# First attention of a gated two-layer block: the next group's key projection in step 3, GpSimd's weight split ahead of a group, the row maximum ahead of step 0's fill

## The reference, cut to what matters

```python
q = (layernorm(x) @ Wq + bq).reshape(B, L, 8, 4, 128)      # B=4, L=256, HID=512
k, v = split(ctx @ Wkv + bkv)                              # 8 key/value heads, 64 context tokens
scores = einsum('blkgd,bmkd->bkglm', q, k) * 128 ** -0.5   # 4 query heads share a key/value head
o = einsum('bkglm,bmkd->blkgd', softmax(scores), v)
x = x + tanh(g) * (o @ Wo + bo)
```

## Time and profile before

| | us |
|---|---|
| median of 3 runs | 1485.03 (1480.28 to 1485.92) |
| profiled execution, device time | 1481.86 |
| its span in the profile | 1480.1 |
| period of a group in the first attention | 40.83 |
| granted TensorE clock, mean of the span | 0.994 |

### The profile page before, as it was taken

The page is one execution under the profiler, slowest core; times in us unless marked ns, Lnnn a source line. Parts: engine busy times, 40 slices in busy tenths (PEclk is TensorE's granted clock), DMA queues, the critical chain, the costliest instruction groups (busy, mean ns, idle before and its releaser), DMA issues.

```text
span 1480.1 us, 24307 instructions
## 1 busy us (share of the span) xinstructions
PE 1394.9 (94%) x7976; PEld 1197.7 (81%) x7976; DVE 1055.5 (71%) x2794; ACT 799.7 (54%) x2210; POOL 464.1 (31%) x590
## 2 busy tenths in 40 slices
PE   4999999998999998999999999999999999999988
PEld 4888888897778877888878878878888888887777
DVE  7777777778632437787777777787787787787775
ACT  4777777776211315565555555555555555664642
POOL 3855555554963612111111111111121111112220
PEclk8999999999999999999999999999999999999999
DMA  4211212111321301001001001001001001010001
GB/s 192 72 62 53 71 71 71 59 69 44 105 68 43 124 1 72 1 1 72 1 1 71 0 1 71 0 1 71 0 1 71 0 1 71 0 43 13 1 8 50
DMA packets 14958, 63.96 MB, mean 43 GB/s; under 512 B 1760, under 2 KB 1760, under 8 KB 10656
## 3 DMA queue, kind: packets, MB, share of 16 engines
q1 hardware_dynamic: 14880, 63.07, 12.0%
HBM read 60.97 MB, written 2.10 MB: 43 GB/s over the span
## 4 chain that ended last, share of the span: by engine, by line
PE 39%; DVE 15%; issue 5%; ACT 4%; DVEq 0%; ACTq 0%
PE psum L57 12%; PE psum L59 11%; PE psum L58 11%; PE psum L1356 2%; PE psum L1450 2%; DVE mx L1041 2%; DVE pT_hi L1014 2%; DVE pT_lo L1010 1%; DVE w1o_lo L1003 1%; DVE p L1056 1%; DVE w1q_lo L1003 1%; ACT pT_hi L1212 1%; DVE dump L1034 1%; DVE oT_lo L1020 1%; DVE v_lo L1071 1%
## 5 line engine op out<-in xcount | busy, mean ns | idle before, releaser
L1289 ACT ACTIVATE p<-psum,nb,rq 128x320 f32<-128x320 f32 x256 | 155.2, 613 | 162.8 <-DVE nb L1045 162.8
L57 PE MATMUL psum<-w1q_hi,xnT_lo 128*128 128x512 f32 x288 | 120.9, 420 | 16.7 <-DVE v_lo L1065 9.0
L978 POOL TENSOR_TENSOR rk<-ssk,rms_eps 128x3 f32<-128x3 f32 x32 | 6.3, 196 | 350.7 <-DVE ssk L1082 350.7
L59 PE MATMUL psum<-w1q_hi,xnT_hi 128*128 128x512 f32 x288 | 113.7, 395 | 0.0
L1010 DVE TENSOR_TENSOR pT_lo<-psum,pT_hi 128x512 fp32r<-128x512 f32 x128 | 88.1, 689 | 35.9 <-ACT pT_hi L1212 34.1
L58 PE MATMUL psum<-w1q_lo,xnT_hi 128*128 128x512 f32 x288 | 112.9, 392 | 0.0
L1041 DVE TENSOR_REDUCE mx<-psum 128x2 f32<-128x640 f32 x128 | 105.0, 820 | 6.1 <-PE psum L59 0.5
L1253 ACT ACTIVATE q_raw<-psum 128x512 f32<-128x512 f32 x64 | 38.2, 597 | 123.6 <-PE psum L59 123.6
L363 DVE TENSOR_TENSOR VW_lo<-psum,VW_hi 64x512 fp32r<-64x512 f32 x128 | 88.0, 688 | 19.0 <-ACT VW_hi L459 17.4
L57 PE MATMUL psum<-w1o_hi,oT_lo 128*128 128x512 f32 x256 | 100.5, 393 | 0.0
L58 PE MATMUL psum<-w1o_lo,oT_hi 128*128 128x512 f32 x256 | 100.3, 392 | 0.0
(11 more groups left out here) (235 smaller groups left out, 4657.6 us busy)
## 6 DMA issues: line engine op xcount, KB each, us to landing
raw_q<-in_w0q SPq DMA_DIRECT2D x8, 1024.0 KB, 4.8
raw_o<-in_w0o SPq DMA_DIRECT2D x8, 1024.0 KB, 4.8
raw_q<-in_w1q SPq DMA_DIRECT2D x8, 1024.0 KB, 7.5
raw_o<-in_w1o SPq DMA_DIRECT2D x8, 1024.0 KB, 4.8
raw_kv<-in_w_gu SPq DMA_DIRECT2D x10, 512.0 KB, 3.6
raw_gu<-in_w_gu SPq DMA_DIRECT2D x10, 512.0 KB, 3.7
raw_kv<-in_w0kv SPq DMA_DIRECT2D x8, 515.0 KB, 3.3
raw_kv<-in_w1kv SPq DMA_DIRECT2D x8, 512.0 KB, 5.5
```

The source lines that it names most:

```text
L57: pe.matmul(out, w[1], m[0], start=start, stop=False)
L59: return pe.matmul(out, w[0], m[0], start=False, stop=stop)
L1289: last = act.activation(k.p1[:, tile, h, :], s_pair(j)[:, h % 2, :], ACT.Exp, bias=k.nb[:, i:i + 1], scale=k.rq[:, i:i + 1], accum_out=k.r ...
```

## The change

Four edits, all in the first attention. The key fill of the next group, ("kv", 0), moves from step 7 to step 3, on PE, ACT and DVE alike; the value fill stays in step 7. The numbers and banks of the fills follow the new order; the last group, which has no next fills, gets an order of its own. POOL copies the bias (now a sum with a tile of zeros) and makes kv hi and kv lo of the next group at the start of its body, ahead of the first scaling; only `q_last` stays behind it, and its wait changes from "all fills up to the group before are drained" to "(kv, 1) of the group now running is drained". On DVE the row maximum comes ahead of the fills in step 0, as in all the other steps.

```diff
-    NEXT_PREP = {7: [("kv", 0), ("kv", 1)], 8: [("wk", 0), ("wk", 1), ("wk", 2)], 9: ...
+    NEXT_PREP = {3: [("kv", 0)], 7: [("kv", 1)], 8: [("wk", 0), ("wk", 1), ("wk", 2)], 9: ...
...
-    ORDER = sum(OWN_PREP.values(), []) + sum(NEXT_PREP.values(), [])
+    ORDER = sum((OWN_PREP.get(s, []) + NEXT_PREP.get(s, []) for s in range(NT + 3)), [])
+    LAST_ORDER = sum(OWN_PREP.values(), [])
...
             if t == 0:                                        # next_ready
-                pool.wait_ge(kv_in, 16 * g + 16)
                 pool.wait_ge(q_in, 16 * g + 16)
-                pool.wait_ge(prep_free, HEAD + FILLS * (g - 1))
...
             if t == 0:                                        # next_split
-                bias_copy(pool).then_inc(bias_in, 1)
                 q_last_row(pool).then_inc(q_row_set, 1)
-                hi_piece("kv", 0)
-                hi_piece("kv", 1)
-            elif t == 1:
-                lo_piece("kv", g, 0)
-                lo_piece("kv", g, 1)
...
+        def split_kv(g, used):
+            pool.wait_ge(kv_in, 16 * g + 16)
+            pool.wait_ge(prep_free, used)
+            pool.tensor_tensor(k.bias[:, :], k.raw_kv[:, KVW:KVW + GH + 2], k.zeros[:, :], ALU.add).then_inc(bias_in, 1)
+            for i in range(CONV["kv"]):
+                hi_piece("kv", i)
+            for i in range(CONV["kv"]):
+                lo_piece("kv", g, i)
+
         def body(g, nxt):
+            if nxt:
+                first = isinstance(g, int) and g == 0
+                split_kv(g + 1, 2 if first else HEAD + FILLS * (g - 1) + ORDER.index(("kv", 1)) + 1)
...
-                if s == 0:                                    # vector, body
-                    for fill in fills:
-                        prep(base, fill)
                 if s < NT:
                     dve.wait_ge(s_full, n + 1)
                     dve.tensor_reduce(k.nb0[:, s % 2, :], by_head(s_bank[s % 2][:, 0:GH * CTX]), AX.X, ALU.max,
                                       negate=True).then_inc(nb_ready, 1)
-                if s > 0:
-                    for fill in fills:
-                        prep(base, fill)
+                for fill in fills:
+                    prep(base, fill, nxt)
```

More of the change, by code:

```diff
@@ L153, in attn0_phase @@
                 4: [("vw", 1, 1)], 5: [("vw", 2, 1)], 6: [("vw", 3, 1)]}
-    NEXT_PREP = {7: [("kv", 0), ("kv", 1)], 8: [("wk", 0), ("wk", 1), ("wk", 2)], 9: [("wk", 3), ("wk", 4), ("wk", 5)],
+    NEXT_PREP = {3: [("kv", 0)], 7: [("kv", 1)], 8: [("wk", 0), ("wk", 1), ("wk", 2)], 9: [("wk", 3), ("wk", 4), ("wk", 5)],
                  10: [("wk", 6), ("wk", 7), ("vw", 0, 0)]}
-    ORDER = sum(OWN_PREP.values(), []) + sum(NEXT_PREP.values(), [])
-    FILLS, OWN = len(ORDER), sum(map(len, OWN_PREP.values()))
+    ORDER = sum((OWN_PREP.get(s, []) + NEXT_PREP.get(s, []) for s in range(NT + 3)), [])
+    LAST_ORDER = sum(OWN_PREP.values(), [])
+    FILLS, OWN = len(ORDER), len(LAST_ORDER)
     HEAD = FILLS - OWN
@@ L171, in attn0_phase, with place @@
     arrived, hi_of, lo_of = {"kv": kv_in, "q": q_in, "o": o_in}, {"kv": kv_hi, "q": q_hi, "o": o_hi}, {"kv": kv_lo, "q": q_lo, "o": o_lo}
-    def place(base, fill):
+    def place(base, fill, nxt=True):
         if base is None:
@@ L177, in place @@
         else:
-            at, slot = base + ORDER.index(fill), HEAD + ORDER.index(fill)
+            i = (ORDER if nxt else LAST_ORDER).index(fill)
+            at, slot = base + i, HEAD + i
         return at, k.bank[slot % 3]
@@ L300, in gpsimd @@
         pool.memset(k.minus_half[:, :], -0.5)
+        pool.memset(k.zeros[:, :], 0.0)
         pool.wait_ge(ident0, 1)
@@ L345, in head_o_hi, with prep @@
             dve.tensor_copy(k.w_o[0][:, :], k.raw_o[:, :]).then_inc(o_hi, CONV["o"])
-        def prep(base, fill):
-            (at, bank), kind = place(base, fill), fill[0]
+        def prep(base, fill, nxt=True):
+            (at, bank), kind = place(base, fill, nxt), fill[0]
             dve.wait_ge(prep_hi, at + 1)
@@ L516, in tensor, with prep @@
     def tensor(pe):
-        def prep(base, fill, g):
-            (at, bank), kind = place(base, fill), fill[0]
+        def prep(base, fill, g, nxt=True):
+            (at, bank), kind = place(base, fill, nxt), fill[0]
             if not (isinstance(at, int) and at < 3):
@@ L552, in body @@
                 for fill in OWN_PREP.get(s, []):
-                    prep(base, fill, g)
+                    prep(base, fill, g, nxt)
                 for fill in NEXT_PREP.get(s, []) if nxt else []:
@@ L578, in body @@
                     if t == 0:
-                        pe.wait_ge(prep_free, base + ORDER.index(("vw", 3, 0)) + 1)
+                        pe.wait_ge(prep_free, place(base, ("vw", 3, 0), nxt)[0] + 1)
                     if t == 4:
-                        pe.wait_ge(prep_free, base + OWN)
+                        pe.wait_ge(prep_free, place(base, ("vw", 3, 1), nxt)[0] + 1)
                     if not (first and t < 2):
@@ L1743, in build @@
             k.w_q, k.w_o = pair(scope, "w0q", [QW]), pair(scope, "w0o", [QW])
-            k.bias, k.q_last = sb(scope, "bias", [GH + 2]), sb(scope, "q_last", [GH])
+            k.bias, k.q_last, k.zeros = sb(scope, "bias", [GH + 2]), sb(scope, "q_last", [GH]), sb(scope, "zeros", [GH + 2])
             k.kvT = pair(scope, "kvT0", [2, BATCH * CTX])
```

## The result

The changed kernel has a median of 1467.95 us (1465.57 to 1468.37, 4 runs) beside 1485.47 us (1480.28 to 1486.25, 4 runs) for the kernel before on the same chip. The ratio is 0.9888, 95% interval 0.9869 to 0.9907: 16.6 us faster by the ratio, between 14 and 19. The forecast was 1469 us. The profiled execution took 1468.23 us with a span of 1466.4; before it was 1481.86 and 1480.1.

What follows compares the result with a forecast made beforehand. PE's order of work sets the pace, with stops of 2.37 us a group to win. 6 x 1.92 + 1.0 + 1.37 = 13.9 us, taken from a mean of 1483.3, gives 1469 us; range for 8 in 10: 1462 to 1477.

Steps and rivals of the forecast that it cites:

- Gap A: PE's stop before S(2), behind tile 0's exponentials: 0.63 us a group, to go with the earlier row maximum.
- gap B: PE's stop between S(3) and tile 1's transposes, for pT lo: 1.74 us a group, to go with both edits.
- The new wait at the wk fill: PE's first wk fill would wait for POOL's last Wq lo piece: 0.45 us a group, about 0.95 in group 0.
- The rival without a new wait: At the wk fill POOL's piece comes early enough: 17.5 us gained, 1466 us; chance 0.10.
- The rival by which the time comes back later: Wq or wk drains hold PE nearly as long as was won: 0 to 5 us gained, near 1481; chance 0.09.
- POOL's split: About 3.9 us of kv work ahead of the first scaling, covered with 4 us; in group 0 no cover.
- the rival by which POOL blocks DVE: In steps 10 and 0 the split locks DVE out, delaying the maximum: +9.5 us, 1493; 0.05 for above 1483.
- the rival by which it fills nothing: ACT or DVE falls behind in step 3, PE waits one tile on: 7.8 us gained, 1475.5; chance 0.14.
- Group 7: The last group, without a key fill, gains 1.37 us by the earlier row maximum alone.
- the full group, 1.92 us: Gain of each of six groups: 2.37 us of PE's stops less 0.45 of wait at the wk fill.

Runs made afterwards that it cites:

- the tile last: Changed kernel with the tile of zeros allocated behind all others, so kvT, WK, VW, p and pT stand where they stood before: 1470.0 us, ratio 0.9896.
- the reordered one: Changed kernel with POOL's last Wq lo piece ahead of the first Wo hi piece at tile 6: 1463.14 us, ratio 0.9852.
- the kernel with the fill first: Changed kernel with the fill put back ahead of the row maximum in step 0: 1474.34 us.
- 128-byte tile: Changed kernel with a tile of zeros of 128 bytes a partition in place of 64: 1466.64 us, single run.
- all shifted: Kernel before the change with 64 bytes allocated ahead of all tiles: 1484.07 us, ratio 1.0001.
- the split late: Changed kernel with POOL's split of kv back behind the first two scalings, key fill in step 3: 1494.55 us, single run.
- the first padded kernel: Changed kernel with POOL's Wq lo piece moved first, plus 64 unused bytes ahead of w_kv and 64 ahead of w_q: 1465.25 us, ratio 0.9868.

## Why the prediction was right, step by step

**Both stops were caused as told.** Gap A and the larger part of gap B came from the late maximum, the rest of gap B could be filled: the maximum alone leaves 6.0 us of the 13.1 waited and gains 1.33 us a group where 1.37 was worked out; the key fill without the maximum leaves 0.1 us of gap B. With both, PE stops at neither. The margin for pT lo of tile 0 is 0.43 us (163.90 against 164.33), where 0.66 was worked out; PE also arrives earlier for being quicker. One tile on, 0.9 was worked out: pT lo of tile 1 ends at 167.10 and PE asks at 167.99.

**The new wait at the wk fill** was put at 0.45 us: PE is free at 181.38 (181.15 and one pace of 0.23), starts at 181.74, and the first matmul after it is slow by 0.11: 0.47. Two of its terms miss in opposite directions: POOL's piece ends at 181.69, so PE comes 0.31 us too soon where 0.23 was worked out, and it starts 0.05 us behind POOL's end where 0.12 was taken from group 0. Most of the first miss is PE's quicker pace again: with the tile last it is 0.25. In group 0 it was put at 0.95: 0.84 idle and about 0.1 of slow restart. The order of POOL's pieces, which takes this wait away, gives 0.51 back. The rival without a new wait fell for this kernel and is what the reordered one does. The rival by which the time comes back later fell too, since nothing but this wait is new.

**POOL's split** is covered in full groups by 4.38 us, where 4 was worked out. In group 0, where it has no cover, POOL's scaling holds the transposes by 0.36 us, as told, and they come at 44.88 (44.95). That the two times agree to 0.1 us means little: over the thirteen traces here they lie anywhere from 44.34 to 45.40. Its durations are the old ones (1.17, 2.56), and the drain of DVE beside it in group 0 is still 1.39 for two. So the rival by which POOL blocks DVE fell. The key fill brought back no wait one tile on: the rival by which it fills nothing fell.

**Group 7** gains by the maximum alone: from the first transposes of group 7, 16.82 us earlier, to the feed-forward, 17.43 us earlier, it is 0.61, where 1.37 - 0.63 = 0.74 was worked out. PE's wait for pT lo there is 1.0 us.

**The term that was mis-sized** is that of the full group, 1.92 us: it measured 2.45, and 2.05 where the tiles stay in their old places. The sum, cut at the first transposes of a group:

| | forecast | measured |
|---|---|---|
| up to group 1's first transposes (group 0's 1.0 and group 1's gap A, 0.63) | 1.63 | 2.11 |
| six full groups | 11.52 | 14.71 |
| from group 7's first transposes on | 0.74 | 0.61 |
| first attention | 13.9 | 17.4 |

Of the 3.5 us that were missed, 2.7 are PE's pace, shown by the kernel with the tile last: 0.40 in each of six groups, and 0.34 from group 0's first transposes to group 1's (39.31 against 38.97). The other 0.13 us a full group are no single error: cut at the transposes, no stretch of the group with the tile last is off the forecast by more than 0.04 us. The forecast took every matmul at the pace of before; the tile of zeros was costed at its 0.2 us sum on POOL, and not as something that moves what lies behind it.

**Where the agreement is luck.** The profiled executions differ by 13.6 us, nearly the forecast 13.9, but this is 17.4 less 3.7 behind the first attention, where the two falls of the clock took 4.2 and 0.5 came back elsewhere. The forecast of 1469 lies 1 us above the median because two misses nearly cancel: 3.5 us too little gain, taken from a mean of 1483.3 where the kernel before then had 1485.47.

## What to carry to other kernels

Two stops of an engine can have one cause upstream: look for the last instruction in the chain that was done in the wrong order, and let the reordered work fill what remains. A fill that is moved takes away the cover of what stood behind it, so work out which piece ends last there; its producer's order may be the next edit (here 0.5 us a group for two swapped lines). An added tile, however small, moves the tiles allocated behind it: compare the pace from start to start of a matmul that should be unchanged before a gain is put down to a schedule. And read a stop from start to start too: in the kernel with the fill first, 0.46 us a group was lost in two places that the list of waits did not name.

## What the runs showed of the hardware that was not expected

The pace of 256-column matmuls on fp32r operands went with how far apart the two operands lie in SBUF. In the kernels where WK's distance from xn is a multiple of 128 bytes (before, maximum alone, tile last, 128-byte tile, all shifted) the mean from start to start is 0.1185 to 0.1193 us; 0.1193 is the one at 0 modulo 256 (the 128-byte tile), the others are at 128. At 192 modulo 256 it is 0.1142 to 0.1152 us in seven kernels (in that with the split late for the groups 1 to 5, at full granted clock), at 64 modulo 256 it is 0.1169 in one (the first padded kernel). w0q against kvT and w_kv against ctxT behave alike (0.119 to 0.116), 512-column matmuls hardly (0.231 to 0.230). Another way of picking the matmuls moves these means by up to 0.0006 us. The Trainium skill (TensorE: Matmul & The Clock Gate, section "Back-to-back issue gap") has the gap of a single matmul as columns / 2.4 + 2.5 ns, 109 ns for 256 columns, and says that at small column counts this leaves out what the weight load takes. The trace agrees in that every mean here lies above it, at 0.114 us or more; but between 0.1146 and 0.1185 us the columns and the loads are the same, and the section has nothing that tells these two apart. What the distance acts on was not found. w_kv's fills moved from 0.1161 to 0.1174 between two kernels in which their own distance is the same, so something else has a part.

The granted clock of the last 123 us was 0.96 in the profiled execution of the changed kernel and 1.00 (2.4 GHz) before, with the same work and PE busy for 90% and 89% of it. The two falls in it cost 1.6 and 2.6 us. What set them off was not found.
